# Storing and reloading the rotated queries at other points of the attention, and splitting the values on another engine

## The reference, cut to what matters

```
q = (hidden_states @ Wq).reshape(b, s, H, D).transpose(0, 2, 1, 3)      # H = 16 heads, D = 64
k = (hidden_states @ Wk).reshape(b, s, HKV, D).transpose(0, 2, 1, 3)    # HKV = 4 groups
v = (hidden_states @ Wv).reshape(b, s, HKV, D).transpose(0, 2, 1, 3)
q = _apply_rope(q, cos, sin)
k = _apply_rope(k, cos, sin)
scores = jnp.einsum('bkgqd,bkpd->bkgqp', qg, k) * scale
scores = jnp.where(causal, scores, jnp.float32(-1e+30))
probs = jax.nn.softmax(scores, axis=-1)
out = jnp.einsum('bkgqp,bkpd->bkgqd', probs, v).reshape(b, H, s, D)
return out @ Wo
```

## Time and profile before

| | |
|---|---|
| median of three runs | 2079.47 us |
| the profiled execution | 2077.51 us |
| its span, first to last instruction | 2075.7 us |
| mean granted TensorE clock | 0.926 of full speed |
| PE matmul busy | 1772.9 us, 85% |
| DVE busy | 1552.2 us, 75% |
| ACT busy | 993.4 us, 48% |
| POOL busy | 886.5 us, 43% |

### The profile page before, as it was taken

The page is one execution under the profiler, slowest core; times in us unless marked ns, Lnnn a source line. Parts: engine busy times, 40 slices in busy tenths (PEclk is TensorE's granted clock), DMA queues, the critical chain, the costliest instruction groups (busy, mean ns, idle before and its releaser), DMA issues.

```text
span 2075.7 us, 26866 instructions
## 1 busy us (share of the span) xinstructions
PE 1772.9 (85%) x8596; PEld 1383.4 (67%) x8596; DVE 1552.2 (75%) x2822; ACT 993.4 (48%) x2129; POOL 886.5 (43%) x1203
## 2 busy tenths in 40 slices
PE   6868799999875879999877779999987687999997
PEld 3756667777764766777665566677776575777776
DVE  4588778885658778888458877888664986888846
ACT  1313276675320437677331326677722043676843
POOL 0061256654224235666215225566511513566531
PEclk9988899999998979999988888999998897999998
DMA  6500334431410053543150024443241004344315
GB/s 234 200 1 1 96 103 120 109 90 47 183 53 1 1 135 90 133 118 73 40 211 1 1 64 125 104 121 98 48 183 57 1 1 122 98 118 118 83 27 203
DMA packets 92203, 187.26 MB, mean 90 GB/s; under 512 B 29119, under 2 KB 44287, under 8 KB 88326
## 3 DMA queue, kind: packets, MB, share of 16 engines
q1 hardware_dynamic: 84742, 171.66, 28.4%
q10 hardware_dynamic: 7296, 13.63, 2.3%
HBM read 129.39 MB, written 45.89 MB: 84 GB/s over the span
## 4 chain that ended last, share of the span: by engine, by line
PE 50%; DVE 21%; POOL 9%; ACT 5%; issue 5%; DVEq 5%; DMA 2%; ACTq 1%; SPq 1%; POOLq 0%
PE ps L387 8%; PE ps L510 5%; PE ps L682 5%; PE ps L530 5%; PE ps L393 5%; PE ps L531 4%; PE ps L549 4%; PE ps L550 4%; PE ps L553 4%; POOL psplit L1310 4%; POOL psplit L1304 4%; DVE psplit L1080 4%; PE ps L723 3%; DVE ps L1070 2%; DVE oT L1091 2%
## 5 line engine op out<-in xcount | busy, mean ns | idle before, releaser
L1070 DVE CUSTOM_DVE_ANT_0 ps<-ps,mrow 128x128 f32<-128x128 f32 (+7 forms) x512 | 381.7, 767 | 91.0 <-PE ps L510 85.3
L1304 POOL TENSOR_SCALAR_AFFINE_SELECT psplit<-psplit 128x256 fp32r<-128x256 f32 x512 | 246.0, 480 | 313.3 <-DVE psplit L1080 285.1
L806 ACT ACTIVATE psplit<-ps 128x512 fp32r<-128x512 f32 (+3 forms) x768 | 372.4, 485 | 0.0
L805 ACT ACTIVATE pT<-ps 128x512 f32<-128x512 f32 (+3 forms) x512 | 256.0, 500 | 163.6 <-PE ps L531 122.5
L530 PE MATMUL ps<-qhh,khl 128*128 128x512 f32 (+3 forms) x768 | 273.2, 356 | 11.8 <-DVE mx L1070 7.1
L549 PE MATMUL ps<-psplit,vhi 128*65 128x512 f32 (+3 forms) x768 | 267.3, 348 | 14.4 <-POOL psplit L1304 13.6
L510 PE MATMUL ps<-khl,qhh 128*128 128x512 f32 (+3 forms) x768 | 239.6, 377 | 42.9 <-DMA qhh<-work 15.7
L531 PE MATMUL ps<-q,k 65*128 65x512 f32 (+3 forms) x768 | 269.6, 351 | 0.0
L553 PE MATMUL ps<-psplit,vhi 128*65 128x512 f32 (+3 forms) x768 | 260.2, 339 | 0.0
L550 PE MATMUL ps<-psplit,vlo 128*65 128x512 f32 (+3 forms) x768 | 260.1, 339 | 0.0
L1310 POOL TENSOR_TENSOR psplit<-pT,psplit 128x512 fp32r<-128x512 f32 (+3 forms) x256 | 223.7, 874 | 14.1 <-ACT psplit L806 13.0
(11 more groups left out here) (176 smaller groups left out, 3390.3 us busy)
## 6 DMA issues: line engine op xcount, KB each, us to landing
qhh<-q_scratch SPq DMA_DIRECT2D x112, 256.0 KB, 5.1
q_scratch<-hrow SPq DMA_DIRECT2D x24, 1024.0 KB, 7.1
mix<-inverse_scratch SPq DMA_DIRECT2D x64, 256.0 KB, 3.6
q<-q_scratch SPq DMA_DIRECT2D x56, 256.0 KB, 4.4
sgn<-sgn_scratch SPq DMA_DIRECT2D x8, 1024.0 KB, 13.4
Kf<-kf_scratch SPq DMA_DIRECT2D x4, 2048.0 KB, 17.4
khl<-k_scratch SPq DMA_DIRECT2D x24, 256.0 KB, 7.9
in_w<-in_w_scratch SPq DMA_DIRECT2D x4, 1536.0 KB, 10.6
```

The source lines that it names most:

```text
L805: A(full(n)[:, 0:hi - lo], ps[:, b, 0:hi - lo], ACT.Exp, scale=SCALE)
L806: A(psplit[:, n % PRING, 0, 0:hi - lo], ps[:, b, 0:hi - lo], ACT.Exp, scale=SCALE)\
L1070: V.tensor_tensor_reduce(out=v, in0=v, in1=mrow[:, L - n:L], scale=1.0, scalar=-3e38, op0=ALU.add, op1=ALU.max, accum_out=mx[:, u % 2, i:i ...
L1304: G.affine_select(out=v, in_=v.bitcast(F32), compare_op=ALU.is_ge, fill=0.0, base=0, pattern=[[0, 2], [1, P]], channel_multiplier=-1).then ...
```

## The change: other places for the stores and for step 4, and the values' low parts on DVE

1. **Values.** The copy into `vfull` is gone from ACT. DVE makes `vlo` straight from PSUM and `vhi`, the first half right before the row maxima of head 0, the second right behind their `negate(0)`. A values bank is free only when DVE is done (`v_done`).
2. **Step 4.** On PE, `project(4)` stands behind `turn_maxima(0)`, and `project_values(1)` ahead of it. On DVE, `rotate(4)` comes behind `value_low(1)`; on POOL in head 0, block 3. `high` and `low` of steps 4 and 5 come three to four blocks later.
3. **Stores.** All stores stand at the end of a head: 4, 5, 6, 7, 8, 9 at the end of heads 0, 1, 3, 4, 7, 8. Behind an odd store SP waits at once until both stores of the group have landed.

```diff
-HIGH_AT = {(0, 4): 4, (1, 2): 5, (3, 9): 6, (4, 9): 7, (7, 9): 8, (8, 9): 9}
-LOW_AT = {(0, 6): 4, (1, 5): 5, (3, 11): 6, (4, 11): 7, (7, 11): 8, (8, 11): 9}
-STORE_LATE = {0: 4, 1: 5}
-STORE_FIRST = {4: 6, 5: 7, 8: 8, 9: 9}
+HIGH_AT = {(0, 7): 4, (1, 5): 5, (3, 9): 6, (4, 9): 7, (7, 9): 8, (8, 9): 9}
+LOW_AT = {(0, 10): 4, (1, 8): 5, (3, 11): 6, (4, 11): 7, (7, 11): 8, (8, 11): 9}
+STORE_IN = {0: 4, 1: 5, 3: 6, 4: 7, 7: 8, 8: 9}
...
-                project(4, QCOL + GQ * HD)
                 for i in range(NT):
                     score_rows(0, i)
+                project_values(1)
                 turn_maxima(0)
-                project_values(1)
+                project(4, QCOL + GQ * HD)
...
-                if n < 2:
-                    act.wait_ge(s["v_done"], n + 1)
...
                       ps[:, b, :].rearrange("p (t g n) -> p t g n", t=2, g=KV), ACT.Copy)
-                    A(vfull(t), ps[:, b, :], ACT.Copy).then_inc(s["v_copied"], 1)
+                      ps[:, b, :].rearrange("p (t g n) -> p t g n", t=2, g=KV), ACT.Copy).then_inc(s["v_high"], 1)
...
+            def value_low(h):
+
+                for t in range(4 * h, 4 * h + 4, 2):
+                    dve.wait_ge(s["v_high"], t // 2 + 1)
+                    b = bk.wait(dve, ("v", t))
+                    V.tensor_tensor(vlo[:, :, t:t + 2, 0:HD].rearrange("p g t n -> p t g n"),
+                                    ps[:, b, :].rearrange("p (t g n) -> p t g n", t=2, g=KV),
+                                    vhi[:, :, t:t + 2, 0:HD].rearrange("p g t n -> p t g n").bitcast(F32),
+                                    ALU.subtract).then_inc(s["v_done"], 1)
...
-                rotate(4)
+                value_low(0)
                 for i in range(NT):
                     row_maxima(0, i)
                 negate(0)
+                value_low(1)
+                rotate(4)
...
                     if u + 2 < HEADS:
-                        if u and (u + 2) % GQ == 0:
-                            for k in (2 * g + 4, 2 * g + 5):
-                                sp.wait_ge(*rope_stored(k))
                         load_query(u + 2)
-                    if u in STORE_FIRST:
-                        store(STORE_FIRST[u])
...
-                    if u in STORE_LATE:
-                        store(STORE_LATE[u])
+                    if u in STORE_IN:
+                        store(STORE_IN[u])
+                        if STORE_IN[u] % 2:
+                            for k in (STORE_IN[u] - 1, STORE_IN[u]):
+                                sp.wait_ge(*rope_stored(k))
```

More of the change, by code:

```diff
@@ L231, in turned @@
         def turned(k):
-            n = k if k < 4 else 1 if k == 4 else 2 + k % 2
+            n = k if k < 4 else 2 + k % 2
             return oT[:, 2 * n:2 * n + 2, :].rearrange("p a n -> p (a n)").rearrange("p (k n) -> p k n", n=HALF)
@@ L255, in full @@
             return pT[:, r, :] if r < FRING - 1 else mix[:, 4:6, :].rearrange("p k n -> p (k n)")
-        def vfull(t):
-            return pT[:, t // 2, :] if t < 4 else oT[:, 0, (t - 4) * D:(t - 2) * D]
         def stored_at(k):
@@ L283, in adaln_hyena_binffn_gqa_moe @@
                  "q_loaded1", "q_loaded2", "q2_loaded0", "q2_loaded1", "k_loaded0", "k_loaded1", "v_done", "nm_done", "nmr_done", "m_loaded0",
-                 "m_loaded1", "v_copied",
+                 "m_loaded1", "v_high",
                  "exp_done", "masked_done", "low_pool", "low_dve", "pv_done", "o_done", "sum_loaded", "inverse_done",
@@ L488, in project_values @@
                 for t in range(4 * h, 4 * h + 4, 2):
-                    b = bk.take(pe, ("v", t), until=(s["v_copied"], t // 2 + 1))
+                    b = bk.take(pe, ("v", t), until=(s["v_done"], t // 2 + 1))
                     for u in range(2):
@@ L835, in value_rows @@
                     A(vhi[:, :, t:t + 2, 0:HD].rearrange("p g t n -> p t g n"),
-                      ps[:, b, :].rearrange("p (t g n) -> p t g n", t=2, g=KV), ACT.Copy)
-                    A(vfull(t), ps[:, b, :], ACT.Copy).then_inc(s["v_copied"], 1)
+                      ps[:, b, :].rearrange("p (t g n) -> p t g n", t=2, g=KV), ACT.Copy).then_inc(s["v_high"], 1)
             def gated_rows(dt):
@@ L881, in _ @@
                     store_rest(2 * h + 1)
+                value_rows(1)
                 turn_maxima(0)
-                act.wait_ge(s["rope_lo"], 1)
-                value_rows(1)
                 for u in range(HEADS):
@@ L1318, in rotate @@
                 G.tensor_tensor(r[:, 1, :], r[:, 1, :], r[:, 2, :], ALU.add).then_inc(s["rope_done"], 1)
[L1320 to L1326, removed]
-                                    ALU.subtract).then_inc(s["v_done"], 1)
             with pool.Fori(0, B):
@@ L1362, in _ @@
                     normed(LN_ATT, h)
-                rotate(0)
                 G.memset(vhi[:, :, :, HD:HD + 1].bitcast(F32), 1.0)
@@ L1369, in _ @@
                 pool.drain()
-                value_low(0)
-                rotate(2)
-                rotate(4)
-                value_low(1)
+                for k in (0, 2):
+                    rotate(k)
                 for u in range(HEADS):
@@ L1379, in _ @@
                             mask(u, c, j)
+                        if (u, n) == (0, 3):
+                            rotate(4)
                         if (u, n) in PROJECT_AT:
```

## The result

| | before | after |
|---|---|---|
| median, us | 2081.66 (2077.51 to 2085.77, 4 runs) | 2112.35 (2111.04 to 2113.77, 4 runs) |
| ratio | 1 | 1.0147 [1.0124, 1.0172] |
| profiled execution, us | 2077.51 | 2113.36 |
| its span, us, and mean granted clock | 2075.7, 0.926 | 2111.6, 0.918 |

The forecast was 2104.5 us, with a range of 2088 to 2120. The two waits forecast in heads 5 and 9 are there at their size. But two other terms of the sum were wrong by 9 and 10 us in opposite directions, so the time is nearer to the forecast than the working deserves. One execution of number 6 stands apart (2488.03 us at a granted clock of 0.642) and is left out of its ratio; the median of the others is 2060.64 us.

The account below looks back on a forecast made before the run. PE was taken as the bound once the heads run, with waits for DVE and DMA at the start. Per batch -2.4 + 0.4 + 8.8 = +6.8 us, four batches +27, from 2077.51 to 2104.5 us; range 2088 to 2120.

Parts of the forecast that it names:

- The two new waits: PE in heads 5 and 9 waits for queries behind stores 7 and 9: 4.4 us each with clock, 8.8 per batch.
- stores 6 and 8: In SP's queue: 1 MB goes ahead of query loads, but nobody waits for these stores for long; no cost charged.
- The start: Each batch up to head 1 and its first blocks: 2.4 us gained per batch, from shorter DVE and ACT chains.
- then the values (3.07): PE, after the eight row matmuls at the start: the values matmuls take 3.07 us, ending at 255.4.
- The wait of 2.14 us: PE at the start of the attention, waiting for the maxima: ready 2.2 us sooner, so this wait goes.
- The banks cost nothing more: At the start: all other takers of a bank find it free earlier than before; no cost.
- Steps 4 and 5 later: High, low and stores 4 and 5 move three or four blocks later: +0.4 us per batch, bounds 0 and +1.5.
- it goes out where it does now: Store 5 stays behind head 0's inverse in SP's queue, so it is still issued at 294.92 us.
- low parts ahead of the queries: SP issues head 3's low parts after the landing wait, before head 4's queries: one issue of 0.6 us.
- Rival 3: Head 1: head 3's queries follow store 4 and come 1 us late, 2.9 us more per batch, 2116 us; chance 0.10.
- Rival 2: Heads 5 and 9: loads arrive before block 8, no new wait; 8 us faster, 2069.5 us; chance 0.06.
- the small term: The +0.4 us per batch for high, low, store 4 and store 5 coming later inside PE-bound heads.

Follow-up runs that it names:

- number 6: Kernel before, only the order moved: project_values(1) ahead of turn_maxima(0), project(4) and rotate(4) behind, values still copied twice: 2061.76 us over all six executions, ratio 0.991.
- Numbers 1 and 2: Kernel before with only the changed SP store order and waits: 2125.73 us, 1.0217; changed kernel with SP's old order and waits: 2070.83 us, 0.9953.
- number 3: Changed kernel, stores still at the ends of heads, waits for landing back before the query loads of heads 2, 6 and 10: 2086.61 us, 1.0031.
- number 10: Changed kernel with SP's order and high/low tables of before, store 5 ahead of head 0's inverse, POOL's rotate(0) ahead of the memsets: 2037.0 us, 0.9797.

## Why the prediction was right, and where it was not

- **The two new waits (+8.8 forecast): right, in mechanism and size.** 8.9 to 9.8 us per batch, waits of 2.53 to 2.93 us. Numbers 1 and 2 switch them on and off. What made it work was a chain found once in the trace (store, landing, load, PE) and a price read from a segment with and without such a wait, clock included. But number 3 shows that even without the wait for landing a store right ahead of the loads costs 16 us in all. The prediction let stores 6 and 8 stand there free of charge, since nobody waits for them. That held for them (no wait in heads 6 and 10), but stores 7 and 9 cost PE a wait of 0.98 to 1.61 us even so.
- **The start (-2.4 forecast, -2.45 and then -5.4 measured): the step is right, the term was mis-sized** by 3 us in three batches. The step that failed is "then the values (3.07)": taken from batch 0 before, where the clock happened to hold; the same matmuls took 5.47 us in the other three batches, and 4.04 to 4.27 after the change. The wait of 2.14 us was priced without the half clock, though the same text charged it to the other waits. Also, the first exponential runs 2.2 us sooner in the batch, not 2.7, and the projections wait 3.46 us and not 3.2: the moved memset took part of it back, and number 10 gives 3.21 without it. "The banks cost nothing more" is wrong as well: the first score rows wait 5.76 us for a bank. And that batch 0 gained just the forecast 2.4 us was luck, since over half of it (1.34 us) came from the clock in head 0's first blocks.
- **Steps 4 and 5 later (+0.4 forecast, +2.6 to +3.1 measured): wrong.** The step that failed is "it goes out where it does now". A place in a queue isn't a time. The store stayed behind the inverse of head 0, and DVE's low parts of step 5 had slipped in front of the reciprocal that the inverse comes from. The second half, low parts ahead of the queries, was priced at the 0.6 us of their issue, less a relief; from store 5 to PE it was 1.14 us.
- **The rivals.** Rival 3, a wait in head 1, did not happen: the rows at 292.76 us have no wait over 1 us. The place was wrong, the idea right: the third wait was the old one before head 4. Rival 2 did not happen; chains under 8.3 us were needed, and these were 11. The Trainium skill's 2.0 us plus bytes over 436 GB/s ("DMA: Bandwidth & Descriptors", section "Anatomy of one DMA — SWDGE (gpsimd) path") makes 4.4 us of a store. The page gives that fit for DMAs issued by GpSimd, and these are SP's: the shortest of 24 took 4.8 us after the change and 4.7 before.
- **The sum (+27 forecast, +29.7 in the profile, +30.7 by the medians)** is close because the start was 9 us too pessimistic and the small term 10 us too optimistic. The range held the time for the right reason in its largest term only.

## What to carry to other kernels

Where one engine is full, price a wait by a segment with it and the same segment without it, in every repetition of the loop and not in the first alone: the clock behind the wait was two fifths of the bill (1.75 of 4.37 us), or more than half (about 1.6 of 2.67 in number 3), or nothing (number 6, batches 1 to 3). A DMA that others wait for should be followed back through its queue to whatever feeds the entry ahead of it; here one store, issued a step sooner, was worth 1.1%, the whole new start of the change 0.5%. And look for loads behind a bulky store in the same queue, whether or not anybody waits for the store itself.

## What the runs showed of the chip that I had not expected

- The granted clock fell to 1.2 GHz behind waits as short as 1.01 us (number 3), and stayed at 2.4 GHz behind others of 1.55 us (number 3, head 11) and 2.48 us (number 6). For the same code in the same batch it differed from one execution to the next. Between two executions of the kernel before, the start of batch 0 took 54.08 and 56.50 us.
- A memset on POOL doubles the time of a DVE tensor_scalar beside it (2.95 us for four, 1.38 without), but leaves a DVE tensor_tensor with two SBUF inputs alone (0.69 us). POOL's subtractions hold up the tensor_tensor by 1.0 us.
